# Two steps of ScalarE in place of VectorE's last step on the gated FP4 tiles, and GpSimd's three passes one slot later

## What is computed

```python
def fp4_quant_dequant(x):                     # BLOCK = 16
    xb = x.reshape(shape[:-1] + (shape[-1] // BLOCK, BLOCK))
    scale = jnp.max(jnp.abs(xb), axis=-1, keepdims=True) / 6.0
    scale = jnp.maximum(scale, jnp.float32(1e-12))
    xn = xb / scale
    idx = jnp.searchsorted(_MID, jnp.abs(xn))          # nearest of the grid
    q = _GRID[idx] * jnp.sign(xn) * scale              # 0 .5 1 1.5 2 3 4 6
    return q.reshape(shape)
...
gate = fp4_linear(x, w_gate)
y = fp4_linear(x, w_up)
h = jax.nn.silu(gate) * y
return fp4_linear(h, w_down)
...
x = x + ga * _L0_attn_ref(h, L0_attn_Wq, L0_attn_Wk, L0_attn_Wv)
h = _layernorm(x, axis=-1) * (1 + cb) + sb
x = x + gb * _L0_ffn_ref(h, L0_ffn_w_gate, L0_ffn_w_up, L0_ffn_w_down)
```

## Time and profile before

| | us |
|---|---|
| median of 3 runs | 669.61 |
| lowest and highest | 666.71, 670.39 |
| the profiled execution, its own time | 664.82 |
| its span, first to last instruction | 663.0 |
| granted TensorE clock, mean | 0.995 |

### The profile page before, as it was taken

One profiled execution on the slowest core, in us unless ns is written; L12 is line 12 of the kernel. 1 busy time (PEld: TensorE's weight loads), 2 busy tenths in 40 slices (PEclk: granted clock), 3 DMA queues, 4 the chain that ended last, 5 costly groups with the idle time before them and its releaser, 6 DMA issues.

```text
span 663.0 us, 11002 instructions
## 1 busy us (share of the span) xinstructions
PE 607.0 (92%) x3758; PEld 478.1 (72%) x3780; DVE 467.8 (71%) x1265; ACT 355.3 (54%) x740; POOL 247.2 (37%) x305
## 2 busy tenths in 40 slices
PE   7977899988878899999989998978999999999997
PEld 5645677876666777886768787766677888777775
DVE  4867689786797456826658978679756674787765
ACT  3424454565545464554346456565566556666554
POOL 4256565454674322004465636457452100000000
PEclk9989999999999999999989999999999999999999
DMA  8300000000000000000000000020000000000111
GB/s 258 97 0 2 1 1 1 1 0 1 1 0 1 1 1 1 1 1 0 1 1 1 1 1 1 0 61 2 0 2 1 1 1 1 1 1 16 33 33 48
DMA packets 12494, 9.65 MB, mean 15 GB/s; under 512 B 1868, under 2 KB 10904, under 8 KB 12440
## 3 DMA queue, kind: packets, MB, share of 16 engines
q1 hardware_dynamic: 12440, 8.95, 4.5%
HBM read 6.84 MB, written 2.10 MB: 13 GB/s over the span
## 4 chain that ended last, share of the span: by engine, by line
PE 67%; DVE 15%; ACT 9%; POOL 4%; issue 4%; DVEq 0%; ACTq 0%; POOLq 0%
PE ps L1007 14%; PE ps L859 11%; PE ps L985 8%; PE ps L1191 5%; PE ps L799 4%; PE ps L1193 4%; PE ps L1192 4%; ACT xn L1359 2%; PE ps L1033 2%; PE ps L1034 2%; PE ps L1051 2%; PE ps L794 2%; POOL rstd L644 1%; PE ps L879 1%; DVE row_max L1836 1%
## 5 line engine op out<-in xcount | busy, mean ns | idle before, releaser
L1425 ACT ACTIVATE probsT<-ps 128x512 f32<-128x512 f32 (+3 forms) x160 | 85.4, 534 | 159.0 <-PE ps L985 159.0
L1007 PE MATMUL ps<-v_sb,probsT 128*128 128x129 f32 (+1 forms) x1124 | 152.0, 278 | 2.6 <-ACT probsT L1427 2.6
L1007 PEld LDWEIGHTS ps<-v_sb,probsT 128*128 128x128 f32 (+1 forms) x1124 | 137.8, 191 | 7.3 <-ACT probsT L1427 4.0
L1836 DVE TENSOR_REDUCE row_max<-ps 128x1 f32<-128x512 f32 (+2 forms) x144 | 87.4, 619 | 53.2 <-PE ps L867 26.7
L985 PE MATMUL ps<-ident,probs 128*128 128x128 f32 (+1 forms) x562 | 90.6, 277 | 16.1 <-ACT hT L1352 7.8
L985 PEld LDWEIGHTS ps<-ident,probs 128*128 128x128 f32 (+1 forms) x562 | 63.6, 139 | 48.0 <-issue 43.6
L1399 ACT ACTIVATE probs<-ps,neg_max 128x512 f32<-128x512 f32 (+7 forms) x158 | 93.1, 621 | 7.7 <-DVE neg_max L1843 7.0
L683 POOL TENSOR_TENSOR hq<-ha,hp 128x352 f32<-128x352 f32 x32 | 29.9, 935 | 100.9 <-DVE hp L1886 100.9
L859 PE MATMUL ps<-k_high,q_high 128*128 128x512 f32 (+5 forms) x100 | 42.5, 425 | 6.9 <-ACT probs L1399 6.9
L643 POOL TENSOR_SCALAR minus_mean<-mv 128x4 f32<-128x4 f32 (+1 forms) x16 | 3.8, 237 | 105.1 <-DVE veps L1586 104.9
L1858 DVE RECIPROCAL rsum<-ps 128x1 f32<-128x1 f32 x64 | 10.5, 164 | 41.6 <-PE ps L1007 41.2
(11 more groups left out here) (294 smaller groups left out, 1399.1 us busy)
## 6 DMA issues: line engine op xcount, KB each, us to landing
out<-x_sb SPq DMA_DIRECT2D x7, 256.0 KB, 2.3
hT_all<-in_L_wmod SPq DMA_DIRECT2D x2, 384.0 KB, 4.5
x_sb<-in_L_attn_x SPq DMA_DIRECT2D x2, 256.0 KB, 3.8
rope_cos<-table_cos SPq DMA_DIRECT2D x2, 256.0 KB, 4.5
rope_sin<-table_sin SPq DMA_DIRECT2D x2, 256.0 KB, 5.6
x_sb<-in_L_attn_x SPq DMA_DIRECT2D x1, 512.0 KB, 6.1
rope_cos<-table_cos SPq DMA_DIRECT2D x1, 512.0 KB, 7.1
rope_sin<-table_sin SPq DMA_DIRECT2D x1, 512.0 KB, 7.3
```

The costliest lines, as they stand in the source:

```text
L1007: mm = pe.matmul(bank(OUT_AT, 0, V_W), probsT[0:size, n % 4, k * P:(k + 1) * P], v_sb[0:size, j, :], start=(c == 0 and k == 0), stop=(c == ...
L1425: ins = act.activation(probsT[:, n % 4, 0:full], bank(TURN, 0, full), ACT.Copy)
L1836: ins = dve.tensor_reduce(dst, ps[:, start:start + width], AX.X, ALU.max, negate=single)
```

## The change

VectorE's quantise now ends with the exponent bits. For the 128x512 groups the last step follows at once on VectorE as before (grid_steps). For the gated tiles it is made by ScalarE in the next slot (hq_steps): relu(0.5 * hp - 0.5), then 2 * ROUND times that, plus ROUND. For hp a power of two this is the same number as max(hp, 1) * ROUND. A column round_at holds ROUND. The two steps stand in ScalarE's slot n + 7 after tanh(n + 1), copy_hq(n - 1) and the exponential of the third chunk. GpSimd's hq_scaled(n) moves from slot n + 6, where it stood behind modulate_1 and q1_low, to slot n + 7, where it stands ahead of both. The semaphore hq_mask tells that VectorE's part is done; hq_grid is now ScalarE's. The wait scales_used is as it was, and so are turn_hq, copy_hq and down.

```diff
@@ GpSimd, loop over the slots
+                    if ffn_tile(s, FFN_LAG + 1) is not None:
+                        hq_scaled(s - FFN_LAG - 1)
                     if at(NORM1_SLOT + 1) is not None:
                         modulate_1(at(NORM1_SLOT + 1))
                     if at(Q1_SLOT) is not None:
                         q1_low(at(Q1_SLOT))
-                    if ffn_tile(s, FFN_LAG) is not None:
-                        hq_scaled(s - FFN_LAG)
@@ ScalarE
+            act.activation(round_at[:], one, ACT.Copy, scale=ROUND).then_inc(round_set, 1)
+            act.wait_ge(round_set, 1)
...
                     if n >= 2:
-                        act.wait_ge(hq_grid, b * TILES + n - 1)
+                        act.wait_ge(hq_mask, b * TILES + n - 1)
                     act.activation(silu_g[:, n % 2, :], bank(GATE, 0, INNER), ACT.Tanh, scale=0.5).then_inc(tanh_ready, 1)
+
+                def hq_steps(n):
+
+                    done = b * TILES + n + 1
+                    act.wait_ge(hq_mask, done)
+                    act.activation(hp[:], hp[:], ACT.Relu, scale=0.5, bias=half[:, 0, 0:1]).then_inc(hq_above, 1)
+                    act.wait_ge(hq_above, done)
+                    act.activation(hp[:], hp[:], ACT.Identity, scale=2.0 * ROUND, bias=round_at[:]).then_inc(hq_grid, 1)
...
                         if c + 2 < n:
                             exp(s, c + 2)
+                        if c == 0 and ffn_tile(s, FFN_LAG + 1) is not None:
+                            hq_steps(s - FFN_LAG - 1)
@@ VectorE
-                    link(dve.tensor_scalar(m.bitcast(I32), a.bitcast(I32), EXPONENT, None,
-                                           ALU.bitwise_and))
-                    last = dve.tensor_scalar(m, m, 1.0, ROUND, ALU.max, ALU.mult)
-                    return last
+                    return dve.tensor_scalar(m.bitcast(I32), a.bitcast(I32), EXPONENT, None, ALU.bitwise_and)
+
+                def grid_steps(m):
+                    return dve.tensor_scalar(m, m, 1.0, ROUND, ALU.max, ALU.mult)
...
-                    quantise(qa[:], qp[:], xn[:, g, :], GROUP * P // BLOCK, qs, scales_used).then_inc(xq_grid, 1)
+                    link(quantise(qa[:], qp[:], xn[:, g, :], GROUP * P // BLOCK, qs, scales_used))
+                    grid_steps(qp[:]).then_inc(xq_grid, 1)
...
-                    quantise(ha[:], hp[:], silu_g[:, n % 2, :], INNER // BLOCK, qh, scales_used).then_inc(hq_grid, 1)
+                    quantise(ha[:], hp[:], silu_g[:, n % 2, :], INNER // BLOCK, qh, scales_used).then_inc(hq_mask, 1)
```

More of the change, by code:

```diff
@@ L352, in build @@
         hp = sb("hp", [P, INNER])
+        round_at = sb("round_at", [P, 1])
         qs = sb("qs", [P, 3, BANK // BLOCK])
@@ L479, in build @@
         hq_grid = sem("hq_grid")
+        hq_mask = sem("hq_mask")
+        hq_above = sem("hq_above")
+        round_set = sem("round_set")
         hq_ready = sem("hq_ready")
```

## The result

The changed kernel takes 700.53 us (median of 4 runs, 697.88 to 704.57); the kernel before took 668.16 beside it (666.66 to 670.39). The ratio is 1.0487, with a 95% interval of 1.0424 to 1.055: 4.9% slower, about 32 us. The profiled execution took 700.31, with a span of 698.5. It is 35.5 above the profiled one of before (664.82), which lay some 3 us under its median.

A forecast was written before the change was run, and what follows sets the result against it. TensorE, busy 92% of the span, was taken as the bound on average. Terms A to E sum to 14.1 us a batch, 28.2 for both, on 664.82: 693.0, stated as 694 us, range 678 to 706.

The forecast's parts named there:

- A: Slots 8 to 11: VectorE's L1879 waits for GpSimd's later passes, so an exponential frees TensorE late; 3.0 us a batch.
- Slots 12 to 15: Slots 11 to 15: GpSimd's passes end before L1879 comes, by 1.1 us in slot 14, so the delay is hidden; nothing.
- B: Slots 16 to 19: L1879 waits for the passes, q_low comes behind them, and TensorE's scores start late; 6.9 us a batch.
- C: Slots 19 and 20: 2.2 us more on VectorE, less 0.8 for GpSimd's norm step; 1.4 us a batch.
- D: Slot 21: GpSimd's passes on tile 14 fall on VectorE's four normalisations; between 0 and 2.4 us a batch, 1.0 taken.
- E: Slot 22: q_low behind ScalarE's steps and GpSimd's passes comes later than the scores stood; 1.8 us a batch.
- Absorbed: Rival: VectorE makes most delays good in its waits, leaving 3.5 us a batch, 672 to 677 in all; chance 0.14.
- ScalarE on top: Rival: ScalarE's steps delay its copy of the second chunk of probabilities by 0.9 us, reaching TensorE; 707 us; chance 0.08.
- Faster: Rival: GpSimd's passes end before L1879 in every slot, saving 3.2 us a batch; 658, by the median 663; chance 0.05.
- ring: VectorE's L1879 of tile n waits for GpSimd's third pass on tile n-1, now in the same slot; 4.1 us chain.

The follow-up runs named there:

- e12: The change for tiles 5 to 8 of each batch alone, the other 12 tiles as in the kernel before: 670.55 us, ratio 1.0039.
- e1: Kernel before with only GpSimd's three passes moved one slot later, ahead of the modulation and q_low; VectorE keeps the grid step: 685.21 us, ratio 1.0262.
- e3: Changed kernel with two buffers, by the tile's parity, for the scaled tile, its grid step and its scales: 694.74 us, ratio 1.0419.
- e2: Kernel before with two more ScalarE activations of 128x352 on scratch tensors, 32 times, nothing waiting for them: 668.70 us, ratio 1.0031.
- e10: Kernel before with GpSimd's passes a slot later, behind the modulation and q_low, and two buffers for scaled tile, grid step and scales: 671.53 us, ratio 1.0049.

## Why the prediction was right

Predicted 694.0 (678 to 706), measured 700.53; the mechanism was the predicted one: L1895 waits 52.8 us for GpSimd's third pass (20 to 50 predicted), VectorE -11.1 and ScalarE +31.1 (-13 and +33 to 38 predicted), and slots 16 to 23 are 15.8 and 13.5 us longer (some 10 predicted). TensorE waits for q_low four times, 5.4 us in sum, instead of twice, 3.1; that the single wait would be longer was wrong (at most 1.5 against 1.7), since TensorE comes to it late itself. A pair of steps is 590 + 589 ns, 1.2 us with the hand-over as estimated. Term by term, for the second batch:

- **Slots 8 to 11 (A), 3.0.** 1.8 in slots 6 to 11. In the first batch the scores that stood at 116.58 start at 121.10; less the 2.4 from before slot 6 that is 2.1 later. L1895 in slot 9 starts at 114.21, by the same count 111.8 where I had 112.7. A little too large. Part of the delay also reached TensorE by a wait that no term held: the turn of tile 2 stands for the third pass itself.

```profile
114.16 0.55 PE L1045 MATMUL ps<-ident,hq 128*128 128x128 f32 x3 [1.04 <-POOL hq L692]
```

- **Slots 12 to 15, nothing.** 0.1; e12 confirms it with 0.3. The reason was right in slots 12 and 14 only: in 13 and 15 VectorE does wait, 1.57 and 3.43, and the delay is made good.
- **Slots 16 to 19, to the scores behind q_low (B), 6.9.** The scores stood at 460.74 in the trace of before and stand at 489.24, a shift of 28.5; 22.2 of it was there at slot 15, so 6.3. The largest term is right by mechanism and, within a tenth, by size. e1 shows the move alone to give it, and e3 shows that two waits share it: opening one leaves the other.
- **Slots 19 and 20 (C), 1.4.** This term was too small. From the scores to slot 20 the shift grows from 28.5 to 32.8: 4.3. The working had "ScalarE, GpSimd and L1879 again" once, 2.2; the trace has it in both slots:

```profile
213.97 0.18 DVE L1895 TENSOR_SCALAR qh<-qh 128x22 f32<-128x22 f32 x1 [2.60 <-POOL hq L692]
...
222.57 0.18 DVE L1895 TENSOR_SCALAR qh<-qh 128x22 f32<-128x22 f32 x1 [2.57 <-POOL hq L692]
```

- **Slot 21 (D), 1.0 of 0 to 2.4, and slot 22 (E), 1.8.** Together 2.9 against 2.8, but made up otherwise. D's lengthening was full. The four normalisations lie beside all three passes and GpSimd's next step; VectorE's row, then GpSimd's:

```profile
227.87 4.02 DVE L1815 TENSOR_SCALAR xn<-x_sb,mv,rstd 128x128 f32<-128x128 f32 x4
```

```profile
227.78 0.94 POOL L687 TENSOR_TENSOR hq<-ha,hp 128x352 f32<-128x352 f32 x1 [5.32 <-ACT hp L1421]
...
229.80 0.78 POOL L692 TENSOR_TENSOR hq<-hq,qh 128x352 f32<-128x352 f32 x1
230.54 1.26 POOL L726 TENSOR_TENSOR h_low<-hT,h_high 128x512 fp32r<-128x512 f32 x1
```

  4.02 us instead of 1.12, and TensorE waited 2.86 for them: above even my upper end, since h_low follows the passes at once. By the Trainium skill, page "SBUF — State Buffer", section "Who interferes with whom", a VectorE instruction in a two-port mode, which a tensor_scalar like this one can enter, and one of GpSimd exclude each other for a whole instruction. The trace agrees: the four normalisations end at 228.80, 229.80, 230.66 and 231.88, each within 0.1 us after one of GpSimd's four (228.71, 229.72, 230.58, 231.80).

  What that wait cost is another matter. When TensorE came to it, it had made good 2.9 of its 16.9 us of delay (the products before it end at 229.17, where they ended at 215.17); the wait took the 2.9 back. And behind the wait the same products, from the turn of the normalised tiles to the turn of the probabilities, took 5.16 us, where they had taken 3.52. Before, then now:

```profile
215.14 0.63 PE L788 MATMUL ps<-ident,xn 128*128 128x128 f32 x4
...
218.06 0.60 PE L985 MATMUL ps<-ident,probs 128*128 128x128 f32 x4
```

```profile
232.03 0.87 PE L792 MATMUL ps<-ident,xn 128*128 128x128 f32 x4 [2.86 <-DVE xn L1815]
...
236.59 0.60 PE L989 MATMUL ps<-ident,probs 128*128 128x128 f32 x4
```

  The granted clock was 0.73 in 230:235 and 0.66 in 515:520, in the second batch, where the same products took 5.16 against 3.51; before it was 1.00 in both places. So 1.6 us in each batch are clock, which no term held. E's wait, for the scores at 244.49, was 1.49 us in the first batch and not 1.8.

The sum predicted was 14.1 a batch; the second batch has 15.4, the first 17.9 from slot 6 on. Of these the clock has 1.6 in each batch and 1.9 more in slot 19 of the first. That the sum came so near is in part luck: A was 1.2 and B 0.6 too large, C was 2.9 too small, and in D and E two things that were left out cancel, the clock and the delay made good ahead of the wait.

The rivals. *Absorbed*: out, a batch loses 15.4 us and not 3.5; only the waits of slots 13 and 15 are made good. *ScalarE on top*: out by e2, 1.9 us. *Faster*: out; L1895 waits in slots 8, 9 and 16 to 20, so the passes end behind its turn there. What the prediction did not see is that its ring was one of two prices for the same lateness: by the same terms I forecast 677 for e3, and that is 18 us wrong.

## What to carry to other kernels

When work moves to an idle engine, count the hand-over by the queue it lands in, not by its length: here ScalarE's two steps, which cost 1.9 us of the run when nothing waited for them (e2), cost 7 to 15 us because GpSimd, in order, waited for them with everything else behind. Before a ring is widened or a step reordered, list all that waits for the same late instruction (here L1895, q_low and the turn of the tile); curing one waiter shows the next, and only the pair told its size. And put time taken off VectorE against time that it then spends beside GpSimd.

## What the runs showed of the hardware

- A VectorE instruction of 0.18 us (128x22, one SBUF input) took 1.15 us at 196.68, beside GpSimd's 128x512 step that ran from 196.54 to 197.80. A short instruction can pay the whole length of GpSimd's.
- In e10 the same 1265 instructions of VectorE were busy 481.3 us against 467.8; the kernel differs from the one before in where GpSimd's passes lie and in the second buffers.
- Four 128x128 normalisations took 4.02 us beside four instructions of GpSimd with less than 0.1 us between them (227.78 to 231.80), and 1.12 us alone: the loss goes on as long as GpSimd's row does.
- TensorE's granted clock fell to 0.50 in 200:205, after a stretch of 5 us with 0.98 us of TensorE's work (195:200). Filling such a wait with products kept it at 1.00 there and bought no time, since something else ended the wait. Behind the 2.86 us wait for the normalisation the lower clock did cost, 1.6 us a batch.
